# Two-layer graph attention: three GpSimd waits for short VectorE steps, a new order of steps on all engines, another list of PSUM banks

## What is computed

```python
def layer0(x, mask):                       # 6 heads of 64
    q, k, v = (heads(x @ W + b) for W, b in ((Wq, bq), (Wk, bk), (Wv, bv)))
    p = softmax(q @ k.T / sqrt(64) + where(mask, 0, -9e15))
    return merge(p @ v) @ Wf + bf

def layer1(x, mask):                       # 12 heads of 32
    h = einsum("bnd,ade->bane", x, W)
    th = tanh(h)
    a = th @ w_src + swap(th @ w_dst)
    a = where(mask, leaky_relu(a, 0.2), -999)
    f = elu(merge(softmax(a) @ h + b))
    gate = sigmoid(x @ H_w.T + H_b)
    return gate * f + (1 - gate) * x

x = layernorm(x + layer0(x, adj))
x = layernorm(x + layer1(x, adj))
```

## Time and profile before

| | |
|---|---|
| runs of the kernel before | 1141.11, 1142.79, 1144.12 us (median 1142.79) |
| the profiled execution's own time | 1140.15 us |
| its span, first to last instruction | 1138.4 us |
| TensorE busy | 1003.7 us (88%) |
| VectorE busy | 1018.4 us (89%) |
| ScalarE busy | 983.8 us (86%) |
| GpSimd busy | 795.1 us (70%) |
| DMA, share of 16 engines | 49.5% |
| granted TensorE clock, mean | 0.970 |

### The profile page before, as it was taken

The page is one execution under the profiler, slowest core; times in us unless marked ns, Lnnn a source line. Parts: engine busy times, 40 slices in busy tenths (PEclk is TensorE's granted clock), DMA queues, the critical chain, the costliest instruction groups (busy, mean ns, idle before and its releaser), DMA issues.

```text
span 1138.4 us, 32966 instructions
## 1 busy us (share of the span) xinstructions
PE 1003.7 (88%) x10570; PEld 826.3 (73%) x10570; DVE 1018.4 (89%) x1969; ACT 983.8 (86%) x2315; POOL 795.1 (70%) x653
## 2 busy tenths in 40 slices
PE   5799999999999999999999999999999999998540
PEld 5778877778787777787777778777777888775320
DVE  6878998999999999999999999999999999999762
ACT  4559998999999999999999999999999999998663
POOL 2146877777787777777777777787777677776664
PEclk9899999999999999999999999999999999999875
DMA  5025653555554445555544555554445555445543
GB/s 199 16 76 119 132 130 93 124 120 144 132 135 124 116 118 122 122 145 130 128 116 106 124 119 145 131 129 126 108 117 123 133 142 128 121 118 104 100 98 83
DMA packets 315187, 136.50 MB, mean 120 GB/s; under 512 B 268944, under 2 KB 310160, under 8 KB 315152
## 3 DMA queue, kind: packets, MB, share of 16 engines
q1 hardware_dynamic: 315152, 136.06, 49.5%
HBM read 30.56 MB, written 12.58 MB: 38 GB/s over the span
## 4 chain that ended last, share of the span: by engine, by line
DVE 39%; issue 25%; PE 13%; ACT 7%; POOL 4%; DMA 2%; DVEq 2%; SPq 2%; ACTq 1%; POOLq 0%
PE gen L502 9%; ACT p_hi L847 3%; DVE z L1189 3%; DVE z_max L1196 3%; DVE sd L1020 3%; DVE stats L1164 2%; DVE y L1160 2%; DMA p1t_lo<-p_lo 2%; DVE k_lo L994 2%; DVE p L1116 2%; DVE stats L1233 2%; DVE q_lo L991 2%; POOL rstd L1393 2%; DVE p_off L1125 2%; DVE x L1184 2%
## 5 line engine op out<-in xcount | busy, mean ns | idle before, releaser
L1405 POOL TENSOR_TENSOR p_lo<-z,p_hi 128x1536 f16<-128x1536 f32 x64 | 199.8, 3122 | 59.0 <-ACT p_hi L847 59.0
L839 ACT ACTIVATE z<-z,z_off 128x128 f32<-128x128 f32 x768 | 231.8, 400 | 0.0
L1361 POOL TENSOR_TENSOR prod<-th,w_sd_rows 128x768 f32<-128x768 f32 x64 | 117.8, 1841 | 47.5 <-ACT th L760 47.5
L1410 POOL TENSOR_TENSOR f<-f,x_kept 128x384 f32<-128x384 f32 x64 | 64.3, 1004 | 92.0 <-DVE f L1228 92.0
L812 ACT ACTIVATE p<-p,p_off 128x128 f32<-128x128 f32 x384 | 118.8, 394 | 1.1 <-DVE p_off L1125 1.0
L666 PEld LDWEIGHTS gen<-h_part,p1t_hi 128*128 128x128 f16 x1536 | 61.5, 96 | 79.8 <-issue 33.5
L666 PE MATMUL gen<-h_part,p1t_hi 128*128 128x33 f16 x1536 | 67.4, 179 | 58.8 <-DMA p1t_lo<-p_lo 46.1
L502 PE MATMUL gen<-W_hi,x1t 128*128 128x384 f16 x384 | 105.8, 331 | 9.1 <-DMA x1t<-x_part 4.9
L1189 DVE SCALAR_TENSOR_TENSOR z<-zp,z 128x1536 f32<-128x1536 f32 x64 | 112.0, 1749 | 1.5 <-ACT z L821 1.3
L1196 DVE TENSOR_REDUCE z_max<-z 128x12 f32<-128x1536 f32 x64 | 111.5, 1742 | 0.0
L502 PE MATMUL gen<-Hw_hi,x1t 128*128 128x384 f16 x384 | 105.2, 329 | 0.0
(11 more groups left out here) (171 smaller groups left out, 3907.1 us busy)
## 6 DMA issues: line engine op xcount, KB each, us to landing
xt_raw<-x_t SPq DMA_DIRECT2D x32, 384.0 KB, 3.4
x_raw<-x SPq DMA_DIRECT2D x32, 384.0 KB, 3.1
x_held<-x SPq DMA_DIRECT2D x64, 192.0 KB, 2.4
x_kept<-x_held SPq DMA_DIRECT2D x64, 192.0 KB, 2.2
out<-out_tile SPq DMA_DIRECT2D x64, 192.0 KB, 1.9
mask_kept<-mask SPq DMA_DIRECT2D x32, 64.0 KB, 1.8
mask<-mask_kept SPq DMA_DIRECT2D x32, 64.0 KB, 1.9
adj<-adj SPq DMA_DIRECT2D x32, 32.0 KB, 1.8
```

Source lines behind the costliest of these rows:

```text
L839: last = act.activation(z[:, g, N * h:N * (h + 1)], z[:, g, N * h:N * (h + 1)], ACT.Exp, bias=z_off[:, g, h:h + 1])
L1361: pool.tensor_tensor(prod[:, g, :].rearrange("p (s d) -> p s d", s=2), th[:, g:g + 1, :].to_broadcast([128, 2, D]), rows["w_sd"][:, :].rea ...
L1405: pool.tensor_tensor(p1_lo[:, g, :], z[:, g, :], p1_hi[:, g, :], ALU.subtract).then_inc(w1_lo[g].sem, 1)
L1410: pool.tensor_tensor(f[:, g, :], f[:, g, :], x1_kept[:, g, :], ALU.subtract).then_inc(f_diff[g].sem, 1)
```

## The change

GpSimd's `value_part3(0)`, `next_x_low` and `first_low` each get a wait ahead of their others: the first two for `features_negative(0)` of the same turn on VectorE, the third for `norm0(1)`. All five engines get a new order of their steps, TensorE's list of bank users follows its new order, and the users are spread over the banks anew. No instruction that computes is added, removed or resized.

```diff
@@ -132,10 +132,10 @@
-GEN_USERS = ("qk1", "qk2", "h0", "ctx1", "qk0", "h1", "pr0", "v0", "ct1", "v1", "f0", "sdt", "pr1", "pt00", "pt01", "g0", "f1", "ctx0", "pt10", "g1", "pt11", "ct0")
+GEN_USERS = ("qk2", "qk1", "h0", "ct0", "qk0", "h1", "ctx1", "pr0", "v0", "ct1", "f0", "sdt", "v1", "pr1", "pt00", "pt01", "f1", "g0", "ctx0", "pt10", "g1", "pt11")
-LATE_USERS = {"f0": 1, "h1": 1, "g0": 1, "f1": 1, "sdt": 1, "z0": 1, "ctx1": 1, "pr0": 1, "ct1": 1, "z1": 1, "g1": 1, "pr1": 1, "h0": 1}
-BANKS = {"f0": 4, "h1": 2, "g0": 3, "qk0": 1, "f1": 2, "sdt": 1, "pt00": 1, "pt01": 4, "ctx0": 1, "pt10": 2, "pt11": 4, "ct0": 1, "ctx1": 2, "v0": 3, "pr0": 4, "ct1": 2, "pr1": 2, "qk1": 3, "h0": 4}
+LATE_USERS = {"f0": 1, "h1": 1, "g0": 1, "f1": 1, "sdt": 1, "z0": 1, "ct0": 1, "ctx1": 1, "pr0": 1, "ct1": 1, "z1": 1, "g1": 1, "pr1": 1, "h0": 1}
+BANKS = {"f0": 3, "h1": 2, "qk0": 3, "f1": 2, "sdt": 2, "pt00": 3, "pt01": 1, "ctx0": 3, "pt10": 2, "ct0": 2, "v0": 1, "pr0": 4, "g1": 1, "qk1": 1, "qk2": 4, "v1": 4}
@@ -468,21 +468,21 @@
+    turn.later(1, keep_x1, 1)
+    turn.late(0, keep_mask)
     turn.later(1, turn_weights1_high, 0)
+    turn.later(1, turn_weights1_low, 0)
+    turn.step(-1, load_transposed_x)
     turn.late(1, hold_x1, 1)
-    turn.late(1, hold_x1, 0)
-    turn.step(-1, load_transposed_x)
-    turn.later(1, turn_weights1_low, 0)
+    turn.step(-1, load_adj0)
     turn.later(1, turn_weights1_high, 1)
+    turn.late(1, targets_flat)
     turn.later(1, turn_weights1_low, 1)
-    turn.late(1, targets_flat)
-    turn.step(-1, load_adj0)
+    turn.step(1, turn_x1, 0)
+    turn.late(1, keep_x1, 0)
     turn.late(-1, load_x)
-    turn.step(1, turn_x1, 0)
-    turn.late(1, keep_x1, 1)
     turn.step(1, copy_mask)
-    turn.late(1, keep_x1, 0)
-    turn.step(0, keep_mask)
+    turn.step(1, hold_x1, 0)
     turn.step(1, turn_x1, 1)
     turn.late(2, store, 0)
     turn.late(2, store, 1)
@@ -669,35 +669,35 @@
+    turn.step(0, queries_keys, 2)
     turn.step(0, queries_keys, 1)
-    turn.step(0, queries_keys, 2)
     turn.late(1, hidden, 0)
-    turn.late(0, attend0, 1)
+    turn.late(0, context_transposes, 0)
     turn.step(0, queries_keys, 0)
     turn.late(1, hidden, 1)
+    turn.late(0, attend0, 1)
     turn.late(0, project, 0)
     turn.step(0, values, 0)
     turn.step(0, scores, 0)
     turn.late(0, context_transposes, 1)
-    turn.step(0, values, 1)
     turn.late(2, attend1, 0, 0)
     turn.late(2, attend1, 0, 1)
     turn.late(2, attend1, 0, 2)
     turn.late(1, source_target_transposes)
+    turn.step(0, values, 1)
     turn.step(0, scores, 1)
     turn.late(0, project, 1)
     turn.step(0, weights0_transposes, 0, 0)
     turn.step(0, weights0_transposes, 0, 1)
-    turn.late(1, gate_rows, 0)
+    turn.late(1, attention1, 0)
     turn.late(2, attend1, 1, 0)
     turn.late(2, attend1, 1, 1)
     turn.late(2, attend1, 1, 2)
-    turn.late(1, attention1, 0)
+    turn.late(1, gate_rows, 0)
     turn.step(0, attend0, 0)
     turn.step(0, weights0_transposes, 1, 0)
     turn.late(1, gate_rows, 1)
     turn.step(0, weights0_transposes, 1, 1)
-    turn.step(0, context_transposes, 0)
     turn.late(1, attention1, 1)
@@ -868,7 +868,7 @@
-    turn.late(1, hidden_tanh, 0)
+    turn.late(0, context_high, 0)
     turn.later(1, weights1_high, 0)
     turn.step(0, queries_keys, 1)
     turn.step(0, queries_keys, 2)
@@ -877,39 +877,39 @@
     turn.late(1, hidden_tanh, 1)
     turn.later(1, z_exponent, 1)
     turn.later(1, weights1_high, 1)
+    turn.later(1, gate_quarter, 0)
+    turn.step(0, value_part1, 0)
     turn.late(0, context_high, 1)
-    turn.step(0, value_part1, 0)
+    turn.later(1, gate_quarter, 1)
+    turn.late(1, source_target_copy)
+    turn.step(0, value_part2, 0)
     turn.step(-1, next_x_high)
-    turn.late(1, source_target_copy)
     turn.step(0, scores_exp, 0)
     turn.step(0, heads_spread, 0)
     turn.step(0, heads_spread, 1)
+    turn.step(0, value_part1, 1)
     turn.late(2, elu_exp, 0)
-    turn.step(0, value_part2, 0)
-    turn.step(0, value_part1, 1)
     turn.step(0, weights0_high, 0, 0)
-    turn.later(1, gate_quarter, 0)
     turn.step(0, weights0_high, 0, 1)
-    turn.later(1, gate_quarter, 1)
-    turn.late(1, hidden_part1, 0)
     turn.step(0, scores_exp, 1)
     turn.step(0, later_weight, "W1")
     turn.step(0, later_weight, "Hw")
+    turn.late(1, z_copy, 0)
+    turn.late(2, elu_exp, 1)
+    turn.step(1, first_high, 0)
+    turn.late(1, gate_tanh, 0)
+    turn.step(1, first_high, 1)
+    turn.step(0, weights0_high, 1, 0)
+    turn.late(1, hidden_part1, 0)
     turn.late(1, hidden_part1, 1)
-    turn.late(2, elu_exp, 1)
-    turn.late(1, z_copy, 0)
-    turn.late(1, gate_tanh, 0)
-    turn.step(1, first_high, 0)
+    turn.step(0, weights0_high, 1, 1)
     turn.step(0, value_part2, 1)
-    turn.step(0, weights0_high, 1, 0)
-    turn.step(0, weights0_high, 1, 1)
     turn.late(1, gate_tanh, 1)
-    turn.step(1, first_high, 1)
-    turn.step(0, context_high, 0)
     turn.late(1, z_copy, 1)
     turn.late(1, z_exponent, 0)
     turn.late(2, norm1, 0)
     turn.late(2, norm1, 1)
+    turn.step(1, hidden_tanh, 0)
@@ -1252,70 +1252,70 @@
+    turn.later(1, z_leak, 1)
     turn.later(1, z_maxima, 1)
-    turn.late(0, context_inverse, 1)
+    turn.late(0, context_low, 0)
     turn.later(1, z_offsets, 1)
-    turn.late(0, context_norm, 1)
     turn.late(1, hidden_raised, 0)
+    turn.late(1, source_target_sums, 0)
+    turn.step(0, queries_keys, 2)
     turn.step(0, queries_keys, 1)
     turn.step(0, weight_top, "W1")
     turn.step(0, weight_top, "Hw")
-    turn.step(0, queries_keys, 2)
     turn.step(0, queries_keys, 0)
     turn.step(0, later_weight, "Wf")
-    turn.late(1, source_target_sums, 0)
+    turn.late(0, context_inverse, 1)
     turn.late(1, hidden_raised, 1)
+    turn.late(0, context_norm, 1)
     turn.late(0, add_residual, 0)
-    turn.late(0, stats0, 0)
     turn.late(1, source_target_sums, 1)
     turn.late(1, source_target_part1)
     turn.late(1, source_target_residue)
     turn.late(1, source_target_part2)
     turn.late(1, source_target_part3)
     turn.step(0, scores_masked, 0)
+    turn.late(2, features_inverse, 0)
+    turn.step(0, value_residue, 0)
+    turn.late(2, features_norm, 0)
+    turn.step(0, scores_max, 0)
     turn.late(0, context_low, 1)
-    turn.step(0, scores_max, 0)
-    turn.late(2, features_inverse, 0)
-    turn.late(2, features_norm, 0)
     turn.late(2, features_negative, 0)
-    turn.step(0, value_residue, 0)
     turn.step(0, scores_masked, 1)
-    turn.late(0, moments0, 0)
+    turn.late(0, stats0, 0)
     turn.step(0, scores_max, 1)
     turn.step(0, biases_and_unit)
     turn.late(0, add_residual, 1)
     turn.late(2, elu, 0)
     turn.late(0, stats0, 1)
+    turn.late(0, moments0, 0)
+    turn.late(0, moments0, 1)
     turn.step(0, weights0_low, 0, 0)
-    turn.late(0, moments0, 1)
+    turn.late(0, variance0)
     turn.step(0, weights0_low, 0, 1)
     turn.late(2, features_inverse, 1)
     turn.late(2, features_norm, 1)
-    turn.late(0, variance0)
     turn.late(2, features_negative, 1)
+    turn.late(0, norm0, 0)
+    turn.late(0, norm0, 1)
+    turn.late(2, elu, 1)
+    turn.late(1, z_leak, 0)
     turn.step(0, value_residue, 1)
-    turn.late(0, norm0, 0)
     turn.step(0, context_inverse, 0)
-    turn.late(2, elu, 1)
+    turn.late(1, z_maxima, 0)
+    turn.late(1, z_offsets, 0)
+    turn.step(0, weights0_low, 1, 0)
     turn.step(0, context_norm, 0)
     turn.step(0, later_weight, "W1")
     turn.step(0, later_weight, "Hw")
     turn.step(0, gate_biases)
-    turn.late(1, z_leak, 0)
-    turn.late(0, norm0, 1)
-    turn.late(1, z_maxima, 0)
-    turn.step(0, weights0_low, 1, 0)
-    turn.late(1, z_offsets, 0)
     turn.late(2, stats1, 0)
-    turn.step(0, weights0_low, 1, 1)
     turn.late(2, stats1, 1)
     turn.late(2, moments1, 0)
     turn.late(2, moments1, 1)
     turn.late(2, variance1)
-    turn.late(1, z_leak, 1)
+    turn.step(0, weights0_low, 1, 1)
     turn.late(2, shift_norm1, 0)
     turn.late(2, shift_norm1, 1)
-    turn.step(0, context_low, 0)
@@ -1370,11 +1370,14 @@
 def value_part3(g):
+    if g == 0:
+        pool.wait_ge(f_min[0].sem, prev(f_min[0]))
     pool.wait_ge(v_done[1][g].sem, now(v_done[1][g]))
     pool.tensor_tensor(v_part[2][:, g, :, 0:E0], v_res[:, g, :].rearrange("p (a e) -> p a e", a=H0),
 def next_x_low():
+    pool.wait_ge(f_min[0].sem, prev(f_min[0]))
     pool.wait_ge(xt_hi_made.sem, now(xt_hi_made))
     pool.tensor_tensor(xt_lo[:, :, :].rearrange("p c n -> p (c n)"),
@@ -1382,6 +1385,7 @@
 def first_low(g):
+    pool.wait_ge(x1_ready[1].sem, prev(x1_ready[1]))
     pool.wait_ge(x1_high[g].sem, now(x1_high[g]))
     pool.wait_ge(x1_turned[g].sem, prev(x1_turned[g]))
     pool.tensor_tensor(x1_part[:, g, 1, :], x1[:, g, :], x1_part[:, g, 0, :], ALU.subtract)\
@@ -1422,26 +1426,26 @@
     pool.wait_ge(out_ready[g].sem, prev(out_ready[g]))
```

(8 more changed lines are left out.)

## The result

The changed kernel takes 1104.72 us (median of four runs, 1103.71 to 1107.87) against 1141.95 us of the kernel before in runs on the same chip: a ratio of 0.968, 95% interval 0.965 to 0.970. That is 1105.8 us (1102.9 to 1108.7) on the 1142.79 us from which the prediction started. The forecast was 1103 in 1080 to 1133. The profiled execution of after is the slowest of the four, 1107.87 us with a span of 1105.7.

What follows compares the result with a forecast made beforehand. VectorE, fullest at 31.21 us a turn, was taken as the bound, then TensorE: 31.03 + 0.55 = 31.6 against 33.02, times 28 turns 40 us less, 1100 profiled, 1103 us as median; range 1080 to 1133.

Steps and rivals of the forecast that it cites:

- VectorE's loss behind GpSimd: VectorE's negatives (1.49 us a turn) and normalisations (0.57) wait for GpSimd; all 2.06 us go, leaving 29.15.
- TensorE as the next bound: With VectorE freed, TensorE's 31.03 us of work a turn is the next bound, ScalarE close behind.
- Which wait does the work: Of GpSimd's three waits only that of `value_part3(0)` works; order removes the normalisation's loss, the other waits are already met.
- (a): TensorE's second-graph logits wait 0.91 us a turn for `z_leak`; bounds 0 and 0.91 after the change, taken as 0.
- The rival that it stays: `z_leak(0)` still comes late and TensorE's 0.91 us wait stays: 32.5 us a turn, 1128 us; chance 0.20.
- (b): TensorE's `attend1(1)` waits 0.51 us for its bank; this goes, new bank neighbours are harmless; bounds 0 and 0.51, taken 0.
- (c): TensorE's `attend1(0)` waits for transposed low weights `p1t_lo`, 0.54 us today; between 0 and 1.3 after, taken as 0.55.
- The ends: Filling and draining, some 106 us in front and 110 behind the steady turns, were left out of the sum.
- The blocked sums of the draining turns: VectorE's blocked step in a draining turn may go too, 2.7 us.
- SyncE's delay of `turn_x1(0)`: `turn_x1(0)` is delayed behind `first_low(0)`; taken as 0, other end 0.9 us ahead of `hidden(0)`.
- The rule on two SBUF inputs: `xt_lo` on GpSimd overlaps VectorE's two-input `elu(0)` by at most 0.2 us a turn, 6 us in all.
- The slower rival: VectorE's third part of the sums (L1042) falls behind GpSimd's `p_lo(1)`: 2.7 us a turn lost, 1179 us; chance 0.11.

Runs made afterwards that it cites:

- Experiment 9: Kernel before with one swap on GpSimd, `value_part3(0)` ahead of `next_x_low`, and no wait added: ratio 1.002 to the kernel before.
- experiment 3: Kernel before with the three GpSimd waits added, in its old order and banks: ratio 0.971 to the kernel before.
- experiment 6: Kernel before with only the two waits for `features_negative(0)`, in `value_part3(0)` and `next_x_low`: ratio 0.979 to the kernel before.
- experiment 7: Kernel before with only the wait of `first_low` for `norm0(1)`: ratio 1.006 to the kernel before.
- Experiment 1: Changed kernel without its three GpSimd waits, new order and banks kept: ratio 0.971 to the kernel before.
- experiment 8: Changed kernel without its three waits and with `next_x_low` back ahead of `value_part3(0)` on GpSimd: ratio 0.977 to the kernel before.
- experiment 2: Changed kernel with only the wait in `value_part3(0)`, those of `next_x_low` and `first_low` removed: ratio 0.971 to the kernel before.
- experiment 10: Changed kernel with `context_low(0)` ahead of `z_maxima(1)` on VectorE and `weights1_low(1)` on GpSimd waiting for `source_target_part3`: ratio 0.978 to the kernel before.
- Experiment 5: Changed kernel with `context_low(0)` moved one place up on VectorE, ahead of `z_maxima(1)`: ratio 1.077 to the kernel before.

## Why the prediction was right, and where its steps were not

**VectorE's loss behind GpSimd: right.** 2.06 us a turn were to go, leaving 29.15; it measures 29.24. Experiment 9, which moves the loss to other steps without removing it, gives no gain at all, and experiments 3 and 6, which remove it and change no order on VectorE, give most of it: this is the cause. It is the negative's 1.49 us that count: the normalisation's 0.57 are worth 0.03 us a turn alone and 0.12 on top (experiments 6 and 7).

**TensorE as the next bound: right in place, its size off.** It was put at 31.03 us of work and measures 30.54. In experiment 3, where TensorE's order is the old one, the busy time is 30.57 too. Of the 0.49 us, 0.07 is the stretch, which was longer than ten turns (30.96 by the cut above). The matmuls' own times sum to nearly the same over ten turns (593.8 us in before, 592.6 in after), so the work is equal. The rest is that in before the matmuls overlap less, and the busy time counts that as work; why they do stays open.

**Which wait does the work: wrong.** The text gave the gain of the negative to the wait of `value_part3(0)` and only the normalisation's to the order. Experiment 1 shows the wait to be idle in time: the new order keeps `xt_lo` behind the negative by itself, with `v_part` ahead of it, and even without that by the new place of `values(1)` (experiment 8). The sum did not depend on it. That the waits of `next_x_low` and `first_low` find their count already met was right (experiment 2).

**(a) The `z_leak` wait: right**, 0.91 taken as 0, and none measured at the products. The rival that it stays did not come.

**(b) The banks: the term that failed.** The old wait, 0.51, went as forecast, but the text took 0 for the new neighbours and named three pairs. It did not name `h1` behind `ct0`, both on bank 2, where the last reader of `ct0` was moved behind two steps of 1.75 us on VectorE. That wait is 0.83 us a turn, above the whole bound of 0 to 0.51. What the turn would be without it no run shows: in experiment 10 it goes and others come.

**(c) `p1t_lo`: too high.** 0.55 taken, none measured in the steady turns. What is left ahead of L666 is 0.37 us a turn of "issue" at the weight load.

**The sum came out for partly wrong reasons.** Predicted 31.03 + 0.55 = 31.6; measured 30.54 + 0.83 = 31.37, in a turn of 31.36. Floor and `p1t_lo` were 0.49 and 0.55 us too high, the bank 0.83 too low; that they nearly cancel is luck. Over 28 turns the gain is 43.1 us on the profiled executions, 40 were forecast.

**The ends, taken as 0: wrong by about 5 us**, 10.4 in the profiled execution of after, in a part that the text left out as unchanged. The blocked sums of the draining turns did not go either: L1033 takes 2.91 and 2.98 us in two of them. Windows of the rear, from L1116 of the last full turn on, of before and of after:

```profile
1028.47:1138.40 109.93, 49.67 (x544) 32.81 (x539) 69.00 (x127) 69.28 (x153) 66.73 (x53) 0.75 0.45 96
```

```profile
988.55:1105.70 117.15, 57.05 (x564) 37.17 (x563) 69.20 (x128) 70.00 (x155) 66.95 (x53) 0.72 0.40 91
```

VectorE, ScalarE and GpSimd do the same there. TensorE has 20 of the program's 10570 matmuls more to do, among them nine of `values(1)`, which in before came ahead of this masking, and is busy 7.4 us longer, at a granted clock of 0.72 against 0.75 (1.00 in the steady turns of both). Steps moved over the cut between two turns lie there too. Since front and rear together are longer in every run of the new order than in any of the old one, the new order with its banks is the cause; which step of it is, no run tells.

**SyncE's delay of `turn_x1(0)`: right for the steady turns.** `hidden(0)` shows no wait.

**The rule on two SBUF inputs: borne out, without effect.** The overlap of `xt_lo` with `elu(0)` was put at 0.2 us at most; it is none, by 0.01 us. Experiment 9 shows what it would be: an `elu` of 2.12 us. So the sentence of the Trainium skill's page "SBUF — State Buffer", section "Who interferes with whom", that a VectorE instruction with two SBUF inputs contends with a GpSimd instruction that reads SBUF, agrees with the trace.

**The slower rival: real and near.** It had 0.11. Experiment 5 turns it on with one swap. It was put at 2.7 us a turn; there 28 turns take 35.31 us each against 31.39, 3.9 us a turn. The sums hold up what reads them besides VectorE, and the granted clock is lower; the two were not told apart.

## What to carry to other kernels

A short VectorE instruction that shows two durations for one shape, the long one ending 0.1 to 0.4 us behind a GpSimd instruction, is a wait that no semaphore shows: sum the difference over a turn, compare it with the next fullest engine, and that is the most that its removal can bring. Whether a wait or a change of order removed it made no difference here, but where two instructions lie apart by a tenth of a microsecond, a wait that costs nothing today is the safer of the two, since any later move can bring the lock back at another step. When banks are spread anew, go through every pair of neighbours on a bank and ask where the last reader of the first now stands; and when steps move over the cut of a software pipeline, cost the drain as well as the turn.

## What the runs showed of the hardware

The block lasts until GpSimd's instruction ends, whatever the size of VectorE's: 48 elements a partition took 3.06 us instead of 0.21 behind a `p_lo` of 3.11. VectorE can get in between two GpSimd instructions that follow without a gap: in experiment 1 the negative ended at 521.43, 0.22 us behind `v_part`'s end, and `xt_lo`, issued at 521.16, was itself stretched from 1.85 to 1.97 us. Not every VectorE instruction is held: in after the statistics (0.55 us) and the maxima (0.93 us), each with one SBUF input, run at 521.97 and 522.43 beside `xt_lo` and take no longer than their groups' means (the maxima 0.94), while L1223 and L1184, also with one SBUF tile to read (L1184 has two values a partition besides), are held. The section "Who interferes with whom" of the Trainium skill's page "SBUF — State Buffer" names `tensor_scalar`, `copy` and `cast` as able to enter a mode that uses both ports; the trace agrees: L1223 and L1184 are `tensor_scalar`, and the cast of L1029 took 2.32 us instead of 0.19 in a draining turn of before.
